# Scores of key differences, cut at zero by ScalarE, joined into VectorE's maxima in the opening of one cross attention

## The reference

```python
def _L2_xattn_ref(x, context, context_mask, q_w, q_b, kv_w, kv_b, proj_w, proj_b):
    ...   # 16 heads of 8, scale = 8 ** -0.5
    q = (x @ q_w + q_b).reshape(b, n, h, d)
    kv = (context @ kv_w + kv_b).reshape(b, s, 2, h, d)
    k = kv[:, :, 0]
    v = kv[:, :, 1]
    attn = jnp.einsum('bnhd,bshd->bhns', q, k) * scale
    attn = jnp.where(context_mask[:, None, None, :], -jnp.inf, attn)
    attn = jax.nn.softmax(attn, axis=-1)
    out = jnp.einsum('bhns,bshd->bnhd', attn, v).reshape(b, n, c)
    return out @ proj_w + proj_b
```

## Time and profile before

| what | value |
|---|---|
| time, median of 3 runs | 5574.75 us |
| lowest and highest of them | 5571.57 and 5584.76 us |
| the profiled execution, from first to last instruction (its span) | 5808.0 us |
| opening of the plain cross (first piece to last piece of half 0) | 2999.14 to about 3063 us |
| its whole opening, to the first units | to about 3070 us |
| pieces and units spread together | to about 4100 us |
| the same opening in the masked cross | from 1444.76 us |

### The profile page before, as it was taken

One profiled execution on the slowest core, in us unless ns is written; L12 is line 12 of the kernel. 1 busy time (PEld: TensorE's weight loads), 2 busy tenths in 40 slices (PEclk: granted clock), 3 DMA queues, 4 the chain that ended last, 5 costly groups with the idle time before them and its releaser, 6 DMA issues. The chain is left out here.

```text
span 5808.0 us, 98536 instructions
## 1 busy us (share of the span) xinstructions
PE 4173.6 (72%) x37548; PEld 1589.1 (27%) x37548; DVE 3745.4 (64%) x10230; ACT 2485.7 (43%) x3203; POOL 793.2 (14%) x988
## 2 busy tenths in 40 slices
PE   5956999655999999998669999999786711153124
PEld 2333444333122222223422222222254310021002
DVE  5454666586999999983469999999335621056213
ACT  2532666543366666665116777777510100010001
POOL 0000000002000000000020000000000067704772
PEclk9977999877799999999769999999898955576567
DMA  0020000225011121110040111111114000000000
GB/s 14 1 66 10 12 16 10 84 114 172 23 29 32 32 78 32 32 28 7 4 140 21 32 33 38 35 32 32 16 42 129 1 11 13 12 1 7 13 12 8
DMA packets 139839, 206.40 MB, mean 36 GB/s; under 512 B 50877, under 2 KB 103452, under 8 KB 137630
## 3 DMA queue, kind: packets, MB, share of 16 engines
q1 hardware_dynamic: 97758, 181.68, 11.4%
q0 software_dynamic: 20480, 10.53, 1.2%
q10 hardware_dynamic: 21128, 7.88, 0.6%
HBM read 152.65 MB, written 47.35 MB: 34 GB/s over the span
## 5 line engine op out<-in xcount | busy, mean ns | idle before, releaser
L1613 ACT ACTIVATE probs<-ps 128x1024 f32<-128x1024 f32 x1632 | 1580.4, 1022 | 615.4 <-PE ps L1551 613.8
L1639 DVE CUSTOM_DVE_ANT_0 junk<-ps,mask 128x512 bf16<-128x512 f32 (+1 forms) x1664 | 1056.7, 678 | 112.7 <-PE ps L1514 73.3
L1639 DVE CUSTOM_DVE_ANT_0 junk<-ps,nothing 128x512 bf16<-128x512 f32 (+1 forms) x1664 | 1026.8, 677 | 46.5 <-PE ps L1514 43.5
L1514 PE MATMUL ps<-kturned,qturned 49*64 49x512 bf16 (+3 forms) x5642 | 905.9, 394 | 106.2 <-DVE maxima L1639 40.7
L1567 PE MATMUL ps<-probs,vstack 128*18 128x512 f32 x6528 | 875.2, 600 | 0.0
L3281 POOL DMA_INDIRECT line<-table,index x640 | 645.9, 1009 | 877.2 <-DVE index L3654 484.6
L1551 PE MATMUL ps<-qturned,kturned 52*64 52x512 bf16 x6528 | 597.4, 391 | 6.6 <-ACT probs L1613 5.0
L1514 PEld LDWEIGHTS ps<-kturned,qturned 49*64 49x64 bf16 (+1 forms) x5642 | 236.3, 102 | 1093.4 <-DVE maxima L1639 709.5
L1538 PE MATMUL ps<-maskT,split 64*128 64x512 bf16 x1632 | 321.8, 384 | 0.0
L1551 PEld LDWEIGHTS ps<-qturned,kturned 52*64 52x64 bf16 x6528 | 186.6, 105 | 340.8 <-issue 255.5
L1639 DVE DVE_READ_ACCUMULATOR2_ANT maxima<- 128x1 f32 x3328 | 276.8, 83 | 0.0
(11 more groups left out here) (722 smaller groups left out, 4807.3 us busy)
## 6 DMA issues: line engine op xcount, KB each, us to landing
vstack<-values_heads SPq DMA_DIRECT2D x128, 229.5 KB, 4.8
mask_raw<-in_mask_BxSxS_if SPq DMA_DIRECT2D x8, 3202.0 KB, 17.4
kturned<-keys_parts SPq DMA_DIRECT2D x384, 54.0 KB
kturned<-keys_parts SPq DMA_DIRECT2D x384, 48.0 KB
table<-lines SPq DMA_DIRECT2D x51, 256.0 KB, 3.4
line<-table,index POOLq DMA_INDIRECT x640
keys_parts<-parts SPq DMA_DIRECT2D x24, 384.0 KB, 2.8
values_heads<-vall SPq DMA_DIRECT2D x2, 3456.0 KB, 12.4
```

What stands on the lines that cost most here:

```text
L1514: last = nc.tensor.matmul(ring(e)[part, 0:hi - lo], qturned[rows, h % 3, m * P + part.start:m * P + part.stop], kturned[rows, h % 2, lo:hi ...
L1613: nc.scalar.activation(probs[:, u % slots].rearrange("p b n -> p (b n)"), k.ps[:, bank:bank + 2, :].rearrange("p b n -> p (b n)"), ACT.Exp ...
L1639: nc.vector.tensor_tensor_reduce(junk[:, at % RING, 0:hi - lo], ring(e)[:, 0:hi - lo], lost, 1.0, -3.0e38, ALU.subtract, ALU.max, maxima[: ...
```

## The change

For the chunks 0, 2, ..., 10 of half 0, and of the first 12 pieces of half 1, in the plain cross only, TensorE no longer scores the keys a of the even chunk but the differences a - b, where b are the keys of the odd chunk beside it. ScalarE writes relu(q.a - q.b) from the bank into one of four f32 buffers (`twins`). VectorE then reads the bank of the odd chunk with that buffer as second input and adds instead of subtracting: q.b + relu(q.a - q.b) = max(q.a, q.b). So one VectorE instruction covers two pieces. There are 48 such pairs in half 0 and 6 in half 1; 8 pieces of half 0 (the chunk of 384) stay as they were.

For that, a new stage (`soft_ends`) behind `end_row` makes two more rows in DRAM: ends cut at -2^24, and the differences of them. `context_sides` makes the differences of keys for the six pairs of groups, splits them in two parts and stores them (`keys_apart`). `cross` holds them in `kapart`, cleared by GpSimd and loaded by SP with 2 and 10 DMAs for a half; every half loads the ten, though only halves 0 and 1 read them, and TensorE waits for them before each half's first piece. The scores of a unit have 53 rows instead of 52, as the uncut ends get a row of their own, in both crosses. The other lines keep their meaning.

The core of the diff:

```diff
 def context_sides(k, ctxT, wk, wv, bk, bv, joins=0):
...                                             # ScalarE, loop over the groups g
+            def high_apart(j):
+                act.wait_ge(apart_ready, j + 1)
+                if j >= 2:
+                    act.wait_ge(apart_stored[j % 2], 16 * (j // 2))
+                nc.scalar.copy(apart_parts[:, j % 2, 0, :], apart[:, j % 2, :]).then_inc(apart_high, 1)
+            def low_apart(j):
+                act.wait_ge(apart_rest, j + 1)
+                nc.scalar.copy(apart_parts[:, j % 2, 1, :], apart[:, j % 2, :]).then_inc(apart_low, 1)
...                                             # VectorE, same loop
+                if joins and g % 2 == 1:
+                    j = g // 2
+                    if j >= 2:
+                        dve.wait_ge(apart_low, j - 1)
+                    nc.vector.tensor_tensor(apart[:, j % 2, :], whole[:, (g - 1) % 3, :], whole[:, g % 3, :], ALU.subtract).then_inc(apart_ready, 1)
...
+                if joins and g >= 2 and g % 2 == 0:
+                    j = g // 2 - 1
+                    dve.wait_ge(apart_high, j + 1)
+                    nc.vector.tensor_tensor(apart[:, j % 2, :], apart[:, j % 2, :], apart_parts[:, j % 2, 0, :], ALU.subtract).then_inc(apart_rest, 1)
...                                             # SP, same loop
+                if joins and g >= 3 and g % 2 == 1:
+                    apart_out(g // 2 - 1)
...
+def soft_ends(k, masked):
...
+        @block.sync
+        def _(sp):
+            sp.dma_start(ends[:], k.ends_dram).then_inc(loaded, 16)
+            sp.dma_start(lost[:].rearrange("j b n -> j (b n)"),
+                         masked[0, 0:2 * JOINS * BANK].rearrange("(j n) -> j n", n=2 * BANK)).then_inc(loaded, 16)
+            sp.wait_ge(softened, 2)
+            sp.dma_start(k.soft_dram, ends[:]).then_inc(stored, 16)
+            sp.dma_start(k.apart_dram, apart[:]).then_inc(stored, 16)
+            sp.wait_ge(stored, 32)
+        @block.vector
+        def _(dve):
+            o = InOrder(dve, order)
+            dve.wait_ge(loaded, 32)
+            nc.vector.tensor_scalar(ends[:], ends[:], -SOFT, None, ALU.max).then_inc(softened, 1)
+            o.step(nc.vector.tensor_tensor(apart[:], lost[:, 1, :], lost[:, 0, :], ALU.subtract))
+            nc.vector.tensor_scalar(apart[:], apart[:], SOFT, None, ALU.mult).then_inc(softened, 1)
...
+def copied(h, i):
+    m, c, a = pieces()[i]
+    return (h == 0 or (h == 1 and i < LEAD)) and c % 2 == 0 and c // 2 < JOINS
...                                             # cross, TensorE
+                    if taken:
+                        pe.wait_ge(apart_loaded[h % 2], 160 * (h // 2 + 1))
+                        if h < 2:
+                            pe.wait_ge(apart_ends_loaded[h], 32)
...
+                src = kapart[rows, h % 2, c // 2 * BANK:(c // 2 + 1) * BANK] if e in twin else kturned[rows, h % 2, lo:hi]
...                                             # cross, ScalarE
+            def ahead(e):
+                _, h, i = e
+                act.wait_ge(ring_filled, ring_at[e] + 1)
+                if twin[e] >= TWINS:
+                    _, before, n = taken[twin[e] - TWINS]
+                    read_wait(act, ("piece", before, n + 2))
+                nc.scalar.activation(twins[:, twin[e] % TWINS, :], ring(e), ACT.Relu).then_inc(ring_free[ring_at[e] % RING], 1)
...                                             # cross, VectorE
+                if e in twin:
+                    return
                 dve.wait_ge(ring_filled, at + 1)
                 ring_wait(dve, e)
+                apart = ("piece", h, i - 2)
+                if apart in twin:
+                    read_wait(dve, apart)
+                    nc.vector.tensor_tensor_reduce(junk[:, at % RING, :], ring(e), twins[:, twin[apart] % TWINS, :], 1.0, -3.0e38,
+                                                   ALU.add, ALU.max, maxima[:, h % 2, 4 * a + m, c:c + 1]).then_inc(ring_free[at % RING], 1)
+                    return
```

More of the change, by code:

```diff
@@ L34 @@
 BIG = 2.0 ** 30
+SOFT = 2.0 ** 24
+JOINS = 6
 MINUS_INF = -1.0e30
@@ L1197, in context_sides @@
         values_stored = s.sem("values_stored")
+        apart_ready = s.sem("apart_ready")
+        apart_high = s.sem("apart_high")
+        apart_rest = s.sem("apart_rest")
+        apart_low = s.sem("apart_low")
+        apart_stored = [s.sem(f"apart_stored{i}") for i in range(2)]
         block = s.block()
@@ L1217, in _ @@
                 act.wait_ge(key_product, g + 1)
+                if g >= 3 and joins:
+                    act.wait_ge(apart_ready, min((g - 3) // 2 + 1, joins))
                 if g >= 3:
@@ L1277, in _ @@
                 sp.wait_ge(parts_stored[i], 16 * ((len(groups) - i + 2) // 3))
+            if joins:
+                apart_out(joins - 1)
+                for i in range(2):
+                    sp.wait_ge(apart_stored[i], 16 * ((joins - i + 1) // 2))
             sp.wait_ge(values_stored, 16 * len(leave))
+def soft_ends(k, masked):
+    nc = k.nc
+    with Stage(nc) as s:
+        ends = s.sb("ends", [KT, P], BF16)
+        lost = s.sb("lost", [JOINS, 2, BANK], mybir.dt.uint8)
+        apart = s.sb("apart", [JOINS, BANK], BF16)
+        loaded = s.sem("loaded")
+        order = s.sem("order")
+        softened = s.sem("softened")
+        stored = s.sem("stored")
+        block = s.block()
+        @block.sync
[14 more added lines that the diff above has]
+            nc.vector.tensor_scalar(apart[:], apart[:], SOFT, None, ALU.mult).then_inc(softened, 1)
 def end_row(k, masked):
@@ L1374, in cross @@
                 last_piece[e[1], ring_at[e] % RING] = e
+    taken = [e for e in steps if e[0] == "piece" and maskT is None and copied(e[1], e[2])]
+    twin = {e: i for i, e in enumerate(taken)}
     with Stage(nc) as s:
@@ L1394, in cross @@
         ends_loaded = [s.sem(f"ends_loaded{i}") for i in range(2)]
+        apart_cleared = s.sem("apart_cleared")
+        apart_ends_loaded = [s.sem(f"apart_ends_loaded{i}") for i in range(2)]
+        apart_loaded = [s.sem(f"apart_loaded{i}") for i in range(2)]
         keys_loaded = [[s.sem(f"keys_loaded{i}{j}") for j in range(2)] for i in range(2)]
@@ L1454, in _ @@
                 keys(h, 0)
+                if taken and h == 0:
+                    sp.wait_ge(apart_cleared, 1)
+                    apart_ends(h)
+                    apart(h)
                 keys(h, 1)
+                if taken and h == 1:
+                    sp.wait_ge(apart_cleared, 2)
+                    apart_ends(h)
+                    apart(h)
                 values(h)
@@ L1492, in stack @@
                 pool.wait_ge(stack_ready, h + 1)
-            pool.wait_ge(cleared, 5)
+            if taken:
+                for h in range(2):
+                    nc.gpsimd.memset(kapart[:, h, :], 0.0).then_inc(apart_cleared, 1)
+            pool.wait_ge(cleared, 6)
             for h in range(HALVES):
```

73 lines of the change are left out of this document (57 added, 16 removed).

## The result

The changed kernel takes 5592.73 us (median of 20 runs), the kernel before 5576.73 us beside it. The ratio is 1.0024, with a 95% interval of 1.0017 to 1.0031, so +13.4 us (9.5 to 17.3). Repeated on another chip it was 1.0014 (1.0004 to 1.0024). The sum was off: +3.5 us was forecast. Set on the 5574.75 us from which the forecast starts, the ratio gives 5588 us, inside the range; the median itself lies 0.7 us above the range's end.

The account below looks back on a forecast made before the run. VectorE was taken to end last at each step of the opening and to be busiest in the units. Terms of -12.2 + 5.5 + 5.0 + 4.6 + 0.6 = +3.5 us on 5574.75 us gave 5578 us, range 5564 to 5592 us.

Parts of the forecast that it names:

- The opening's chain: Opening: refilling three banks sets 1.99 us per group of four pieces instead of 2.44, a gain of 12.2 us.
- soft_ends: New stage behind end_row: a load, three small VectorE operations and a store, all on the path, +5.5 us.
- context_sides: Stage that writes keys: added subtractions, copies and six stores of differences lengthen it by 5.0 us.
- the start: Start of the opening: two ends and 12 difference DMAs ahead of the first piece on SP, +4.6 us.
- the reason I gave: Stage that writes keys: DMA bytes set its end, with four of six stores falling in the full tail.
- the rest: Masked cross: two more ends ahead of its start, +0.55 us, entered as 0.6 us in the sum.
- the one on later halves: Units: ten loads per later half stay hidden and their bytes disturb nothing; 47 us if that cover were gone.
- what would show it: Signs in the changed profile: groups of 1.99 us, clock 0.50 until the units, opening 12 us shorter, units unchanged in length.
- Rival A: Opening: the clock rises to 2.4 GHz, a group takes 1.78 us, net -2.1 us, 5572.6 us; chance 0.2.
- Rival B: Stage that writes keys: stores add up in sequence, it grows by 24 us, net +22.5 us, 5597 us; chance 0.08.
- Rival C: Opening: VectorE alone sets it, gain 33 us, costs at their low ends, net -22.5 us, 5552 us; chance 0.03.
- TensorE's floor: Opening: four matmuls of 0.427 us limit a group to 1.71 us while the clock stays, capping the gain at 19.7 us.

Follow-up runs that it names:

- t_banks7: The changed kernel with seven PSUM banks in turn in the plain cross's opening instead of three; ratio 0.9981 to the kernel before.
- s_no_wait: The changed kernel with all loads kept, but TensorE waiting for them in halves 0 and 1 only; ratio 1.0005 to the kernel before.
- s_before_wait: The kernel before plus one already satisfied wait on TensorE's queue at each half's start from half 2 on, plain cross; ratio 1.0018 to the kernel before.
- r_two_loads: The changed kernel with key differences loaded and waited for in halves 0 and 1 only; ratio 1.0005 to the kernel before.
- r_prep: The kernel before with the change's preparation and 53rd row, but every piece by the old path; ratio 1.0017 to the kernel before.
- t_wait_20: The kernel before plus a satisfied TensorE wait ahead of piece 20 of each half from 2 on; ratio 0.9999 to the kernel before.
- t_lean7: The changed kernel with ends made inside end_row, differences for two halves only, half 0's loads on ScalarE's queue, seven opening banks; ratio 0.9974 to the kernel before.

## Why the prediction was right in its call and wrong in its sum

**The opening's chain held.** The chain over three banks gave 1.99 us a group and 12.2 us in all; it is 2.01 us and 11.0 us. That the banks were what bound it is shown by t_banks7.

**The preparation held, term by term.** soft_ends +4.8 for +5.5, context_sides +4.8 to +6.1 for +5.0, the start +4.1 to +4.6 for +4.6. The DMA share of the last stretch of context_sides went from 0.87 to 0.94 at 293 GB/s, which agrees with the reason I gave; no run left the stores out, so the reason is not shown. Of the +0.6 us of the rest, the start of the masked cross shows 0.1 to 0.7 us, and 2 us in one profile.

**The step that failed** is the one on later halves: "The ten loads for later halves ... their bytes disturb nothing", and in what would show it, "The stretch of units keeps its length". The first clause is right, as s_no_wait shows. But the step priced the loads and their bytes, and left out the instruction that they bring to TensorE, the wait on apart_loaded at each half's first piece. I looked at whether that wait could be unsatisfied (47 us) and put it at nothing when satisfied. It makes one more semaphore instruction run behind the end of ScalarE's copy of the turned queries, for which TensorE stands idle for 1.0 us at the start of each half. That costs 0.15 us in each of 14 halves and, with the drops of the clock that follow, 8 to 10 us. s_before_wait shows it alone, s_no_wait shows it removed. With this term the sum would have been +11.5 to +13.9 us, and +13.4 was measured. Rows 2 spoke for it: with VectorE busy for 953 and TensorE for 921 of 1000 us there is little slack in which a later start of TensorE could disappear.

**Rival A (the clock rises in the opening)** did not happen: 0.50 at three banks and at seven. The rule of the Trainium skill that a busy TensorE is released (TensorE: Matmul & The Clock Gate, Part 1) is not borne out for this opening by any run here: the clock stayed at 0.50 with 61.70 us of recorded matmuls in 64.70 us before and 47.91 in 52.70 us after. **Rival B (the ring in the stage that writes keys)** did not happen: the stage is 6 us longer at most, far from 18. **Rival C** was rightly not in force, but one of its reasons was wrong. I set TensorE's floor at 4 x 0.427 = 1.71 us a group; t_banks7 runs at 1.22 us and the same clock, since a pair of pieces shares the 0.427 us. Three banks were the only bound, as the chain said. With more banks C's 33 us are almost there: 71.7 - 40.9 = 30.8 us.

**What stays open.** Why the clock falls at some half starts and not at others: the position differs between profiles of kernels with the same wait, and one or two drops came within the units of kernels without it (r_two_loads, r_prep, t_wait_20, t_lean7). That the wait brings them is shown by 6, 7, 6, 6 and 6 drops with it against 1, 1, 2, 2, 1, 2, 1 and 2 without, those where the last half begins counted in; how 0.15 us more of idle time do that, is not. Nor is it shown why the drop there is missing in the kernels with the wait, which gives back 1.3 us. Two waits in the same place, or the wait at a single half, would have told more, and were not tried.

## What to carry to other kernels

A wait that is always satisfied can be an instruction all the same: count it where it stands beside a wait on which the engine is idle, look in the trace for semaphore instructions that run when that idle time has ended, and put it elsewhere (twenty pieces later it was free here). Before saying that an engine is a floor, ask whether its instructions use different parts of it: the records of two matmuls in different rows overlapped here. And where a ring of buffers sets a stage, look for buffers that are idle in that stage only: four free banks were worth 20 us on top of the change, nearly twice what moving half of the work to another engine was.

## What the runs showed of the hardware that was not expected

- One satisfied semaphore wait ahead of a matmul lengthened the gap behind another engine's result from 0.07 to 0.22 us, as a second semaphore instruction ran in it, and 14 of them cost about 9 us (1089.6 against 1080.9 to 1081.1 us), most of it through drops of the granted clock. With it, a half with a drop took 1.0 to 1.8 us more than the same half before.
- Matmuls of 49 rows kept the granted clock at 0.50 through 40 us in which TensorE was recorded as busy for 32.60 us, while the units' matmuls behind them raised it to 1.00.
- Two matmuls of 512 columns in rows 0 to 48 and in rows from 64, into different banks, took 0.43 us together at a clock of 0.50.
- A second DMA queue beside SP's moved the first piece of the opening by 0.9 us only, though the last issue it waits for came 8.8 us behind SP's first one instead of 12.7.
